# Third layer's state-space stage: every third state's drive from TensorE, its first half in the bank of B's row

## The reference, cut to what matters

```python
proj = jnp.einsum('btd,pd->btp', x, in_proj_w)       # x_inner, z, B_param, C_param, delta_raw
xc = silu(causal depthwise convolution of x_inner + conv_b)
delta = softplus(delta_raw @ dt_proj_w.T + dt_proj_b)
A = -jnp.exp(A_log)
def step(h, inp):
    d_t, b_t, c_t, xc_t = inp
    dA = jnp.exp(A[None, None, :] * d_t[..., None])
    h = dA * h + d_t[..., None] * b_t[:, None, :] * xc_t[..., None]
    y = jnp.einsum('bis,bs->bi', h, c_t)
    return (h, y)
y = ys + D_param * xc
out = jnp.einsum('bti,di->btd', y * jax.nn.silu(z), out_proj_w)
```

## Time and profile before

| what | value |
|---|---|
| median of 3 runs | 5335.22 us (5332.41 to 5345.41) |
| profiled execution | 5330.66 us, its span 5328.6 us |
| mean granted TensorE clock | 0.907 |
| PE busy in the span | 4395.1 us (82%) |
| PEld | 2710.1 us (51%) |
| DVE | 3533.3 us (66%) |
| ACT | 2766.8 us (52%) |
| POOL | 2506.6 us (47%) |
| state loop of the stage | 2896.7 to 3824.7 us of the span |

### The profile page before, as it was taken

How to read it: one execution, slowest core, us unless ns; L and a number is a source line. 1 busy time by engine, 2 the same in 40 slices (tenths; PEclk the granted TensorE clock), 3 DMA queues, 4 the chain that set the end, 5 groups by cost and what they waited for, 6 DMA issues and landing times. The chain is left out here.

```text
span 5328.6 us, 109199 instructions
## 1 busy us (share of the span) xinstructions
PE 4395.1 (82%) x42504; PEld 2710.1 (51%) x42504; DVE 3533.3 (66%) x6837; ACT 2766.8 (52%) x4982; POOL 2506.6 (47%) x2343
## 2 busy tenths in 40 slices
PE   8768999999999999677854888887798879985779
PEld 6545666666666666434632343443365444423445
DVE  4347777777777777386455999999764426646646
ACT  4326666666666666463334666565464415542322
POOL 7537666666666666252164766766533310001100
PEclk8789999999999999887866999999999959996889
DMA  1010100101011000000000000000000000003000
GB/s 24 16 30 14 32 20 20 33 21 32 22 29 24 16 16 20 7 1 3 12 0 15 1 0 0 1 0 1 15 1 1 5 14 5 17 1 75 5 21 7
DMA packets 92004, 76.98 MB, mean 14 GB/s; under 512 B 30999, under 2 KB 74279, under 8 KB 90727
## 3 DMA queue, kind: packets, MB, share of 16 engines
q1 hardware_dynamic: 89447, 68.95, 5.2%
q0 software_dynamic: 2048, 1.05, 0.1%
HBM read 40.18 MB, written 1.18 MB: 8 GB/s over the span
## 5 line engine op out<-in xcount | busy, mean ns | idle before, releaser
L4220 POOL TENSOR_TENSOR l_attn_read<-l_attn_state,l_attn_c_rows 128x1024 f32<-128x1024 f32 x256 | 604.5, 2362 | 292.3 <-DVE l_attn_state L4122 174.2
L2595 PE MATMUL psum<-l_ffn_wq,l_ffn_xsT 128*128 128x512 f32 x1152 | 605.5, 608 | 106.9 <-DVE l_ffn_t L2870 101.7
L3006 POOL TENSOR_TENSOR l_ffn_t<-l_ffn_t 128x512 f32<-128x512 f32 x384 | 486.9, 1268 | 417.6 <-DVE l_ffn_t L2870 413.0
L3842 PE MATMUL psum<-l_attn_read,ident 128*128 128x512 f32 x1024 | 489.5, 596 | 7.3 <-DVE l_attn_yz L4130 5.0
L2866 DVE TENSOR_TENSOR l_ffn_t<-psum,l_ffn_tab 128x512 f32<-128x512 f32 x384 | 260.5, 678 | 324.6 <-ACT l_ffn_sq L2746 305.5
L3012 POOL TENSOR_TENSOR l_ffn_t<-l_ffn_t,l_ffn_ss 128x512 f32<-128x512 f32 x384 | 400.3, 1043 | 62.7 <-DVE l_ffn_ss L2885 62.6
L2746 ACT ACTIVATE l_ffn_sq<-psum 128x512 f32<-128x512 f32 x384 | 225.3, 587 | 288.0 <-PE psum L2595 285.6
L4122 DVE TENSOR_TENSOR_SCAN l_attn_state<-l_attn_decay,psum 128x1024 f32<-128x1024 f32 x144 | 328.9, 2284 | 4.5
L2643 PEld LDWEIGHTS psum<-l_ffn_pT,l_ffn_v 64*64 64x64 f32 x3072 | 231.8, 134 | 167.3 <-ACT l_ffn_pT L2768 133.0
L3998 ACT ACTIVATE l_attn_decay<-l_attn_dt,l_attn_a 128x1016 f32<-128x1016 f32 x256 | 292.9, 1145 | 36.0 <-DVE l_attn_state L4119 32.6
L4023 ACT COPY l_attn_c_rows<-psum 128x512 f32<-128x512 f32 x256 | 149.4, 584 | 298.5 <-PE psum L3833 260.1
(11 more groups left out here) (917 smaller groups left out, 11304.0 us busy)
## 6 DMA issues: line engine op xcount, KB each, us to landing
l_ffn_vx<-l_ffn_v SPq DMA_DIRECT2D x192, 128.0 KB, 2.3
l_ffn_wq<-in_L_ffn_Wqkv SPq DMA_DIRECT2D x6, 1536.0 KB, 6.3
l_xattn_toep<-s4d_taps SPq DMA_DIRECT2D x4, 2048.0 KB, 17.5
l_ffn_wo<-in_L_ffn_Wo SPq DMA_DIRECT2D x6, 512.0 KB, 3.9
l_ffn_w<-in_L_ffn_W SPq DMA_DIRECT2D x6, 341.0 KB
l_ffn_w<-in_L_ffn_w SPq DMA_DIRECT2D x3, 512.0 KB, 4.0
x_all<-in_x SPq DMA_DIRECT2D x4, 256.0 KB, 4.6
l_attn_k<-l_attn_dense_k POOLq DMA_DIRECT2D x64, 16.0 KB, 1.9
```

The source lines that it names most:

```text
L2595: nc.tensor.matmul(ring[it % 2], xsT[:, n % 2, m % G, :], w, start=True, stop=True).then_inc(itemed, 1)
L3006: nc.gpsimd.tensor_tensor(t1[:, m % G, i, :], t1[:, m % G, i, :], t2[:, x % 3, :], ALU.add).then_inc(added, 1)
L3842: last = nc.tensor.matmul(total[:, h * GT:(h + 1) * GT], K.ident[:], read[:, k % 3, h * GT:(h + 1) * GT], start=(n == 0), stop=(n == N - 1 ...
L4220: nc.gpsimd.tensor_tensor(read[:, k % 3, :].rearrange("p (h n) -> p h n", h=2), state[:, k % 3, :].rearrange("p (h n) -> p h n", h=2), row ...
```

## The change

`BY_PE` becomes every third state from 3 to 60, 20 of 64. The first drive half of such a state goes to bank 4, where B's row lies, the second to bank 2; both may be written earlier than before. B's row after such a state must wait for that state's first half scan. TensorE's order around these states is written anew.

```diff
-    BY_PE = (3, 6, 9, 12, 17, 25, 33, 41, 46, 49, 52, 55, 58, 61)
+    BY_PE = tuple(range(3, 63, 3))
...
+        pe_drive = (b_bank, K.psum[:, HW:HW + GT])
...
                     if k >= 1:
                         pe.wait_ge((driven, c_moved)[m], k if m else rows_before(k))
+                    if m == 0 and k >= 1 and by_pe(k - 1):
+                        pe.wait_ge(halved, split_before(k - 1) + 1)
...
                     if h == 0:
                         pe.wait_ge(diag_ready, pe_before(k) + 1)
+                        pe.wait_ge(driven, rows_before(k))
+                    else:
                         pe.wait_ge(halved, split_before(k - 1) + 1)
-                    else:
-                        pe.wait_ge(scanned, k)
                     for i in range(G):
-                        last = nc.tensor.matmul(drive[:, h * GT + i * T:h * GT + (i + 1) * T], duT[:, g % 2, h, i, :], b_diag[:, pe_before(k) % 2, i, :],
+                        last = nc.tensor.matmul(pe_drive[h][:, i * T:(i + 1) * T], duT[:, g % 2, h, i, :], b_diag[:, pe_before(k) % 2, i, :],
...
                     if k + 1 < NS and by_pe(k + 1):
+                        drive_half(k + 1, 0)
                         row(k + 1, 1)
                         add(k - 2, 0)
-                        drive_half(k + 1, 0)
                         drive_half(k + 1, 1)
-                        row(k + 2, 0)
+                        add(k - 2, 1)
+                    elif g < NG and by_pe(k):
+                        add(k - 2, 0)
+                        row(k + 1, 0)
+                        row(k + 1, 1)
                         add(k - 2, 1)
                     else:
-                        if k + 1 < NS and not (g < NG and by_pe(k)):
+                        if k + 1 < NS:
                             row(k + 1, 0)
...
+                            source = pe_drive[h] if by_pe(k) else drive[:, at]
-                            nc.vector.tensor_tensor_scan(state[:, k % 3, at], decay[:, k % 3, h, :, :].rearrange("p g t -> p (g t)"), drive[:, at], 0.0,
+                            nc.vector.tensor_tensor_scan(state[:, k % 3, at], decay[:, k % 3, h, :, :].rearrange("p g t -> p (g t)"), source, 0.0,
```

## The result

The changed kernel takes 5364.79 us (median of 7 runs, 5357.15 to 5367.42), the kernel before 5338.96 in the runs beside it (the median of six; a seventh, 5874.12 us, fell in the chip's slow state and is left out). The ratio on record is 1.0053, with a 95% interval from 1.0043 to 1.0063: slower by some 28 us. The forecast was 0.16% slower, with a time within 0.3% of no change as the likeliest case; the measured time lies at the upper end of its range, and the loss is three times the +9 us of its sum.

The account below looks back on a forecast made before the run. VectorE was taken to set the pace, waiting only for TensorE. On the profiled 5330.66 us, -53 + 36 + 30 - 1 - 3 = +9 gave 5340, or 5344 on the median's basis; range 5320 to 5366.

Parts of the forecast that it names:

- VectorE's own share: State loop: 24 conversions save 33 us, existing pairs losing their wait and overlapping scans save 20: -53 us.
- The chain: TensorE's ordered work from VectorE's drive to B's row outlasts VectorE's; next full state's drive waits 0.49 us, 74 times: +36 us.
- The jobs in the chain: TensorE's work for the next group, now between a TensorE-driven state's drive and B's row, delays VectorE: +30 us.
- Part 4: Remaining effects: table-load waits -1 us, a wait at state 33 -3 us; ScalarE's and GpSimd's work hidden.
- Part 1: VectorE's saving in the state loop from conversions, removed 0.30 us waits and overlapping half scans: -53 us.
- half clock: Rival: matmuls behind the longest pause, before drive half 0, run at the lower clock, +4.2 us a period; chance 0.08.
- ScalarE's table loads: They delay C's copies; the wait at state 51 was taken as 3.0 us: -1 us for three groups, bounds -6 and +6.

Follow-up runs that it names:

- e1: The changed kernel with B's row after a TensorE-driven state issued one iteration earlier, ahead of the jobs and one half add; 0.9918 of the kernel before.
- e9: e1 with C's row of the next state moved behind B's row in round 50 only; 5275.74 us, 0.9895 of the kernel before.
- e5: The changed kernel with the next group's jobs that stood behind the iteration before a TensorE-driven state issued one iteration earlier; 0.9996 of the kernel before.
- e8: The changed kernel with one matmul of zeros in TensorE's pause before the first drive half, at six rounds of three groups; 1.0037 of the kernel before.

## Why the prediction was right or wrong, point by point

- **VectorE's own share (-53 us): right.** In e1's and e9's last group, where VectorE waits for TensorE nowhere, 212.9 us stand against 226.5: 13.6 a group, 54 in four.
- **The chain (0.49 us a period, 36 in all): right in place and nearly in size.** The drives wait 0.63 after the last scan, 0.53 above the usual 0.10; 74 of them would make 39. There are 77: behind the scale step, which the prediction let cover the wait whole, three drives still wait 0.2 to 0.6 us. The period was to be 10.11 us and is 10.11. The exact match has some luck in it: TensorE starts 0.15 after VectorE's end and VectorE 0.04 after the row's, where 0.10 was taken for each.
- **The jobs in the chain (30 us): right.** VectorE's drives behind a job of two matmuls wait 1.49, 0.86 more, and in e5 the drives' waits fall by 29.4 us. Chain and jobs together: 80.7 us of waits less the usual 0.10 each are 73 us, where 66 were forecast.
- **What failed: Part 4, the other waits of P's scan halves for TensorE, put at -4 us.** Before, they were 30.1 us, of which the usual 0.30 of 53 states, already counted in Part 1, make 15.9: 14.2 were left. After, they are 26.7: +12.5 us in place of -4, the largest part of the 19 us by which the loop exceeds the forecast. Part 4 let slow matmuls only vanish (-3) or stay behind the table loads. They came in new places.
- **The clock: the step behind it.** At 33 to 39 six waits of 1.3 to 1.5 us came, 8.7 us, and e8, which shortens the pauses, gives 9.8 back; state 54's three waits, 4.1 us, stand behind matmuls of the same slowness. The rival "half clock" had a chance of 0.08 and a price of 4.2 us a period; here only a part of each chain ran slow, at some 1.5 us. The prediction said that the trace of before does not bear such a clock out, going by the stretch with gaps of 0.7 us. The same trace does, at state 33 of the second group, which Part 4 took for a wait like that of the table loads:

```profile
3248.29 3.65 PE L3872 MATMUL psum<-l_attn_b_diag,l_attn_duT 128*128 128x128 f32 x16 [1.56 <-DVE l_attn_state L4119]
...
3240.00:3254.00 14.00, 10.44 (x35) 6.01 (x34) 11.80 (x10) 7.21 (x12) 10.03 (x6) 0.88 0.00 1
```

  TensorE had paused 1.56 us for VectorE, not for ScalarE; 16 drive matmuls then took 3.65 us, not 2.18, at a granted clock of 0.88 in the 14 us around them. The new order has a pause of 1.42 us before the first drive half of nearly every P in the last group, and of 1.88 or more at states 30 to 39 in each of the others. The Trainium skill (TensorE: Matmul & The Clock Gate, section "A second HAM failure mode: psum-queue depth-cycling"), which the prediction set aside, tells of a kernel in which short idle spells between groups of matmuls, with banks cycled, make the clock swing between its levels. The trace agrees at these places (0.83 over 10 us) and not in the last group (1.00).
- **ScalarE's table loads: mis-sized.** The wait at state 51 was to be 3.0 us a group and is 3.8 to 4.0: 3 us in all, part of it slow matmuls again (1.5 to 1.7 us for the second drive half, not 1.05).
- **How the 19 us are made up.** VectorE's share -54, drives' waits +73 and half scans' waits +12.5 are 31; the loop grew by 28.4. The 3 us between overlap in ways that I do not part. Against the forecast the three are -1.4, +7 and +16.5.

The sum was one of a large gain and a large loss, -57 and +66; the chain, the jobs and VectorE's share each came within about a tenth, but the difference that was left, +9, was smaller than the terms forgotten. The range's upper end, drawn for the chain's bounds, held the time by luck: the time came there for another reason.

## What to carry to other kernels

When an operation is moved in an in-order queue, write down the cycle through both engines (here: VectorE's drive, TensorE's list, VectorE's next drive) and add what stands in the list, the occasional jobs too; the wait that the change removes is only one arc of it. One line's place was worth 65 us here, more than the 53 that all the conversions promised. And before ruling out a slow clock, look in the trace at hand at every place where the engine had a longer pause, and at those places alone: the mean over a stage hides it. Moving work out of the way needs the same look at who waits for that work: later jobs and later C rows each gave back what they had won.

## What the runs showed of the hardware that I had not expected

TensorE's granted clock fell to 0.83 in a stretch of 10 us where the engine was busy 8.1 us and had one long pause, of 1.88 us, and stayed 1.00 over a stretch with that pause cut to 1.02 us by one call of zeros; the same pause six states earlier left the drive at 1.13 us, and pauses of 1.42 us all through the last group left the clock at 1.00. In the kernel before, a pause of 1.56 us was followed by drive matmuls of 3.65 us instead of 2.18. So the length of the last pause alone does not tell here whether the clock falls. Four half scans in a row, each with its waits met, take 4.55 us where two pairs with a wait between take 2.33 each: each starts about 0.08 us before the one before it has ended.
